# A decoder after three small attentions: the self-attention's keys in three float32r products, their weights' parts made a layer ahead, the feed-forward weights loaded for every pair

## The chip, the core and the metric

The kernel runs on one core of one Trainium2 chip, as one program. The metric is the device time of one execution in microseconds (us), the median of the runs. All data is float32 outside; "float32r" is a rounded form of float32 in which TensorE takes a product in one pass. A float32 matrix is split into a high part (its float32r rounding) and a low part (the rest, again in float32r), and a product is then high·high + low·high + high·low: three float32r products in place of one float32 product.

Engines are called PE (TensorE), DVE (VectorE), ACT (ScalarE), POOL (GpSimd) and SP (SyncE, which only issues DMAs here). POOL issues DMAs too, from its own queue.

## The reference

x is (8, 112, 256), the context (8, 375, 128).

```
x = attend(x, ctx, L0) + x                       # one head of 256, softmax over the 375 context rows
x = layernorm(attend over queries(x, ctx, L1) + x) * gamma + beta     # softmax over the 112 rows
x = attend(x, ctx, L2) + x
for each of 6 layers:                            # 16 heads of 64
    tn = ln(x);  x = mha(tn, tn, sa_kv, sa_q, sa_ow, mask 112x112) + sa_ob + x
    tn = ln(x);  x = mha(ctx, tn, ca_kv, ca_q, ca_ow, context mask) + ca_ob + x
    tn = ln(x);  x = x + relu(tn @ w1 + b1) @ w2 + b2       # 256 -> 1024 -> 256
```

## The kernel before, in words

The batch of 8 is worked in 4 pairs (NB = 2 batches each, 224 token columns). There are three parts, each with its own counts of how often each PSUM bank is filled and emptied (`Place`): the front part (FRONT_LOOP, the three small attentions n = 0, 1, 2, each over the four pairs u), a start (START, the first pair's self-attention of layer 0 and its feed-in), and the main loop (MAIN_LOOP) of 6 x 4 = 24 iterations, one for each layer and pair. In one iteration a pair gets the self-attention's output rows, the cross-attention and the feed-forward network, and, interleaved with it, the next pair gets its self-attention's keys, queries, scores and sums, so that PE has work while other engines do softmax. The order in each engine's queue is written out by hand; engines wait for each other through semaphores.

The pieces that the change touches:

- **Weight parts.** The self-attention's query and value weights are used in the main loop as parts. In the front part, 24 rounds make them, for all layers: SP loads 128 rows of a weight (0.5 MB) into `w_vq` (`load_raw`, line 374, DMA line 376), POOL makes the high part (line 533) and the low part (line 535) (`parts_of_weights`), SP stores both (1 MB) to a tensor in HBM (`store_parts`, DMA line 381) and waits for the store before it issues a load again. Two places of `w_vq` take turns. POOL works off 16 of the 24 rounds ahead of the rstd computations of n = 1 (`PARTS_BEFORE_NORM`, `inverse_std`, line 522, which DVE's normalisation waits for), and 8 behind them. In the main loop POOL issues one load of 2 MB for the queries and one for the values in each iteration (`load_parts`, line 540).
- **Keys.** The next pair's keys, 8 chunks of 128 columns, are plain float32 products of `w_k` (loaded once a layer) and `tnT_next_full`; they are put between the cross-attention's score tiles at the steps t = 1, 2, 3, 4, 6, 7, 9, 10 of 28 (`KEY_STEPS`). The queries' 8 chunks follow at later steps and are already three float32r products (`projected_in_parts`). A score tile t is three float32r products of 376 columns into one of two banks; PE waits, before tile t, until DVE has taken the maximum of tile t - 2 out of its bank (line 1559). DVE's queue for a step is: maximum of t, reciprocal of t - 1, transposition of tile t - 3 (line 1577), and the odd key chunks' copies (line 1411).
- **Feed-forward weights** `f_1`, `f_2` have SBUF of their own and are loaded once a layer, at its last pair's end.
- **POOL in an iteration**: residual plus bias (line 583), the context pair's high and low part (lines 587, 590), rstd after the self-attention (520, 522), a bias (525), the queries' load (540), then 28 multiplications of a tile of probabilities by 1/sum (602), the values' load, and the next self-attention's part.
- **The front part's end.** For n = 1 DVE, pair by pair, adds PE's bank to the residual (line 1372), takes statistics (1270, 1277), and normalises the pair before (`front_normalise`: two `tensor_scalar` of 256 columns, line 1284, a product with gamma and a sum with beta, 512 columns each, lines 1324 and 1326). After n = 2 it copies each pair to `t_all` (1383) and zeroes the masked columns of the context (1388), four times; PE, SP and DVE itself wait for all four (`front_done`). Then the START part's statistics, rstd and normalisation of the first pair follow, and PE's first transposition.

## Time and profile before

| | |
|---|---|
| median of 3 runs | 2946.46 us (2946.38 to 2948.57) |
| the profiled execution: its own time | 2949.26 us |
| its span, first to last instruction | 2947.4 us |
| mean granted TensorE clock | 0.988 |
| PE busy | 2802.5 us (95%), 24232 matmuls |
| DVE / ACT / POOL busy | 58% / 44% / 37% |
| DMA | 248.56 MB, mean 84 GB/s |
| chain that ended last | PE 84%, DVE 5%, DMA 3% |

"Busy" is an engine's time inside instructions; matmuls are pipelined, so PE's 95% is no peak. The chain is followed back from the last instruction to whatever released each step. The main loop starts at about 290.55 us of the span and each of its iterations takes about 110.17 us (POOL's line 583 at 1399.08 and at 1509.23).

### The profile page before, as it was taken

The page shows a single profiled execution, that of the slowest core. Times are in us where ns is not written, and L with a number is a line of the kernel's source. Part 1 is how long each engine was busy: PE and PEld are TensorE (multiplying, and loading weights), DVE is VectorE, ACT ScalarE, POOL GpSimd, SP SyncE. Part 2 cuts the span into 40 slices and gives each one's busy share as a digit, 9 for nine tenths or more (in the row PEclk, how much of TensorE's full clock was granted, in tenths as well). Part 3 has the DMA queues.
Part 4 walks back from the last instruction along what each step waited for, and adds up shares of the span by engine and source line. Part 5 has one row for each costly group of instructions (what it writes and reads, how often), then busy time and mean ns, then how long its engine had stood idle before and what let it go on. Part 6 is the DMA issues. An engine that isn't in the chain of part 4 may idle for free.

```text
span 2947.4 us, 63938 instructions
## 1 busy us (share of the span) xinstructions
PE 2802.5 (95%) x24232; PEld 2340.4 (79%) x24232; DVE 1705.6 (58%) x6436; ACT 1304.4 (44%) x4273; POOL 1082.8 (37%) x1265
## 2 busy tenths in 40 slices
PE   6767999999999999999999999999999999999999
PEld 4545888888888888888888888888888888888887
DVE  2344656656656656656656655655655655655655
ACT  2223445445444444444444444444444444444444
POOL 2552333433433433433433333333333333333333
PEclk9978999999999999999999999999999999999999
DMA  6645022133222133222133222133222133222120
GB/s 202 241 185 189 32 83 58 35 112 98 67 81 58 40 107 99 74 73 57 49 98 99 82 65 58 56 91 99 88 59 58 62 85 101 88 57 57 59 57 14
DMA packets 148055, 248.56 MB, mean 84 GB/s; under 512 B 16733, under 2 KB 122790, under 8 KB 141478
## 3 DMA queue, kind: packets, MB, share of 16 engines
q1 hardware_dynamic: 140838, 143.79, 18.0%
q0 software_dynamic: 6912, 100.67, 9.4%
q8 instruction: 195, 3.19, 0.5%
q14 instruction: 110, 0.90, 0.1%
HBM read 218.35 MB, written 26.08 MB: 83 GB/s over the span
## 4 chain that ended last, share of the span: by engine, by line
PE 84%; DVE 5%; DMA 3%; POOL 2%; issue 2%; SPq 2%; ACT 1%; DVEq 0%; POOLq 0%; ACTq 0%
PE proj L645 18%; PE sum L966 16%; PE score L645 13%; PE proj L665 9%; PE sum L665 9%; PE sum L645 6%; PE proj L987 3%; PE score L819 2%; PE sum L843 2%; PE proj L924 2%; PE tr L830 1%; PE tr L924 1%; POOL rstd L522 1%; PE tr L966 1%; PE proj L637 1%
## 5 line engine op out<-in xcount | busy, mean ns | idle before, releaser
L602 POOL TENSOR_TENSOR prob<-prob,rtotal 128x375 f32<-128x375 f32 x672 | 543.4, 811 | 685.7 <-DVE rtotal L1568 684.7
L1043 ACT ACTIVATE prob<-prob,negmax 128x375 f32<-128x375 f32 (+1 forms) x686 | 417.7, 609 | 444.0 <-DVE negmax L1559 414.1
L966 PE MATMUL sum<-pT,ctx 32*128 32x224 f32 (+1 forms) x4608 | 500.6, 358 | 15.1 <-DVE qcT L1551 15.1
L966 PE MATMUL tr<-pT,ctx 32*128 32x224 f32 (+1 forms) x4608 | 500.7, 358 | 0.0
L966 PEld LDWEIGHTS sum<-pT,ctx 32*128 32x128 f32 (+1 forms) x4608 | 417.9, 185 | 68.3 <-issue 62.8
L1559 DVE CUSTOM_DVE_ANT_0 prob<-score,cbias 128x375 f32<-128x375 f32 x672 | 357.1, 531 | 186.3 <-PE score L645 180.4
L966 PEld LDWEIGHTS tr<-pT,ctx 32*128 32x128 f32 (+1 forms) x4608 | 417.0, 185 | 0.0
L645 PE MATMUL score<-ctx_parts,qc_high 128*128 128x376 f32 x1344 | 390.9, 372 | 0.0
L1577 DVE STREAM_TRANSPOSE pT<-prob 128x384 f32<-128x384 f32 x672 | 372.6, 558 | 0.0
L564 POOL TENSOR_TENSOR prob<-prob,rtotal 112x448 f32<-112x448 f32 x200 | 186.4, 932 | 452.3 <-DVE rtotal L1426 452.3
L1122 ACT ACTIVATE prob<-prob,negmax 112x112 f32<-112x112 f32 x800 | 298.8, 377 | 85.5 <-DVE negmax L1444 85.5
L645 PEld LDWEIGHTS score<-ctx_parts,qc_high 128*128 128x128 f32 x1344 | 222.0, 189 | 59.3 <-issue 57.2
L645 PE MATMUL score<-ctx_parts,qc_low 128*128 128x376 f32 x672 | 224.8, 335 | 0.0
L1444 DVE CUSTOM_DVE_ANT_0 prob<-score,sbias 112x112 f32<-112x112 f32 x800 | 167.3, 270 | 35.4 <-PE score L819 34.9
L645 PE MATMUL proj<-pT,w_k 128*128 128x224 f32 x768 | 176.4, 352 | 0.0
L645 PE MATMUL proj<-tnT,f 128*128 128x224 f32 x768 | 165.1, 363 | 11.0 <-ACT tnT L1104 11.0
L1129 ACT ACTIVATE v<-proj 112x512 f32<-112x512 f32 x50 | 29.9, 598 | 322.2 <-PE proj L645 322.2
L645 PE MATMUL sum<-tnT,c_q 128*128 128x224 f32 x768 | 162.0, 359 | 0.0
L645 PEld LDWEIGHTS proj<-tnT,f 128*128 128x128 f32 x768 | 135.6, 189 | 26.7 <-issue 15.5
L645 PEld LDWEIGHTS sum<-tnT,c_q 128*128 128x128 f32 x768 | 138.6, 189 | 18.4 <-issue 13.3
L1122 ACT ACTIVATION_READ_ACCUMULATOR prob<-prob,negmax 112x1 f32 x800 | 151.4, 189 | 0.0
L645 PEld LDWEIGHTS proj<-pT,w_k 128*128 128x128 f32 x768 | 140.1, 189 | 1.1
(241 smaller groups left out, 5090.4 us busy)
## 6 DMA issues: line engine op xcount, KB each, us to landing
w_vq_parts<-sa_v_parts POOLq DMA_DIRECT2D x24, 2048.0 KB, 9.1
w_vq_parts<-sa_q_parts POOLq DMA_DIRECT2D x24, 2048.0 KB, 8.5
ctx<-ctx SPq DMA_DIRECT2D x192, 176.0 KB
sa_q_parts<-w_vq_parts SPq DMA_DIRECT2D x12, 1024.0 KB, 5.7
sa_v_parts<-w_vq_parts SPq DMA_DIRECT2D x12, 1024.0 KB, 5.2
f<-ff_w SPq DMA_DIRECT2D x12, 1024.0 KB, 8.4
cmask<-ctx_mask SPq DMA_DIRECT2D x24, 375.0 KB, 4.3
w_k<-sa_kv SPq DMA_DIRECT2D x6, 1024.0 KB, 5.5
```

Of the source, the lines that this page charges most:

```text
L564: pool.tensor_tensor(pr, pr, rtotal[0:S, G * g:G * g + G].unsqueeze(2).broadcast_to([S, G, S]), ALU.mult)\
L602: pool.tensor_tensor(row, row, rtotal[:, G * SG + i:G * SG + i + 1].broadcast_to([P, S2]), ALU.mult).then_inc(prob_ready, 1)
L645: ins = pe.matmul(bank[0:w.shape[1], 0:m.shape[1]], w, m, start=k == 0, stop=k == len(weights) - 1)
L665: ins = pe.matmul(bank[0:S, col:col + E], a, w, start=k == 0, stop=k == len(terms) - 1)
L924: ins = pe.matmul(bank[:, i * T2:(i + 1) * T2], c_kT[rows, c + i, :], qcaT[rows, c + i, :], start=True, stop=True)
L966: ins = pe.matmul(bank[:, 0:HT * R], ctx4[keys_of, m // (HALVES // NB), j, :], pT[keys_of, m % 2, :, j * R:(j + 1) * R], start=j == 0, sto ...
L987: ins = pe.matmul(bank[n * D:(n + 1) * D, c % 2 * T2:(c % 2 + 1) * T2], c_v[:, h * D:(h + 1) * D], cT[:, :, h * S:(h + 1) * S], start=True ...
L1043: act.activation(o, i, ACT.Exp, bias=negmax[0:rows, col:col + 1], scale=scale, accum_out=total[0:rows, col:col + 1]).then_inc(exp_ready, 1)
L1122: ins = act.activation(row, row, ACT.Exp, bias=negmax[0:S, col:col + 1], scale=-1.0, accum_out=total[0:S, col:col + 1])
L1444: ins = dve.tensor_tensor_reduce(out=prob[0:S, k % PROBS, h * S:(h + 1) * S], in0=banks[name][0:S, h * S:(h + 1) * S], in1=sbias[:, g // G ...
L1559: dve.tensor_tensor_reduce(out=prob[:, t % PROBS, 0:S2], in0=banks[name][:, 0:S2], in1=cbias[:, t // TB, :], scale=-SCALE, scalar=3.4e38, ...
L1577: dve.transpose(pT[:, m % 2, i % HT, :], prob[:, i % PROBS, 0:S2B]).then_inc(turned, 1)
```

## The change

1. The key weights get parts too, and the keys are three float32r products, like the queries (`projected_in_parts` with `w_kf_parts`). START's keys stay float32, from a raw copy in `stage`.
2. The parts are made a layer ahead: 6 rounds (layer 0: value, query, key weights, two halves each) in the front part, and in each of the layers 0 to 4 two rounds in each of the first three iterations for the layer after, 30 rounds in 15 iterations. They use one small buffer `stage` instead of two places in `w_vq`, so that load, making and store follow one another.
3. `w_kf` holds the key parts or, later in the iteration, `f_1` and `f_2`: the key parts are loaded by POOL at each iteration's start (2 MB, `load_parts(it + 1, "sa_k", ...)`), the feed-forward weights by SP in each iteration once PE has finished the keys (2 x 1 MB).
4. All 6 front rounds stand ahead of n = 1's rstd; `front_normalise` becomes four `scalar_tensor_tensor` of 256 columns for a pair.
5. The context is masked during n = 2, behind DVE's `sum1` copies; the last residual sums go straight to `t_all`; START's first statistics and normalisation stand between them; `front_done` is gone and PE and SP wait for the last sum instead.

```diff
-    IN_PARTS = [(l, name) for l in range(L) for name in ("sa_q", "sa_v")]
-    ROUNDS_OF_PARTS = EK * len(IN_PARTS)
-    PARTS_BEFORE_NORM = EK * 8
+    IN_PARTS = [(l, name) for l in range(L) for name in ("sa_v", "sa_q", "sa_k")]
+    LAYER_ROUNDS = EK * len(IN_PARTS) // L
+    ITERATION_ROUNDS = 2
+    def rounds_in(it):
+        l, p = it // PAIRS, it % PAIRS
+        if l == L - 1 or p * ITERATION_ROUNDS >= LAYER_ROUNDS:
+            return ()
+        first = LAYER_ROUNDS * (l + 1) + ITERATION_ROUNDS * p
+        return tuple(range(first, first + ITERATION_ROUNDS))
-        w_k = sb("w_k", [P, EK, HDIM])
+        w_kf, w_kf_parts = in_one_place("w_kf", "w_kf_parts", [P, 2, EK, HDIM])
+        stage, stage_parts = in_one_place("stage", "stage_parts", [P, 2, HDIM])
+        f_1, f_2 = w_kf[:, 0, :, :], w_kf[:, 1, :, :]...
...
# SP
+            def load_raw(r):
+                (l, which), k = IN_PARTS[r // EK], r % EK
+                if r > 0:
+                    sp.wait_ge(parts_stored, 16 * r)
+                sp.dma_start(stage[:, 1, :], whole_of[which][l, k * P:(k + 1) * P, :]).then_inc(loaded["stage"], 16)
+            def store_parts(r):
+                sp.wait_ge(parts_ready, r + 1)
+                sp.dma_start(stored_parts[IN_PARTS[r // EK]][:, :, r % EK, :], stage_parts[:, :, :].bitcast(f32))...
-            load_w_k(0)
+            load_first(w_vq[:, 1, :, :], "sa_q", "first_w_q")
+            load_first(w_vq[:, 0, :, :], "sa_v", "first_w_v")
+            load_raw(0)
...
-            sp.wait_ge(front_done, PAIRS)
+            for r in range(LAYER_ROUNDS):
+                store_parts(r)
+                if r < LAYER_ROUNDS - 1:
+                    load_raw(r + 1)
+            sp.wait_ge(parts_stored, 16 * LAYER_ROUNDS)
+            load_first(stage[:, :, :], "sa_k", "first_w_k")
+            sp.wait_ge(taken["proj1"], Place(START).emptied("proj1", 0))
...
+                for r in rounds[0:1]:
+                    store_parts(r)
+                    load_raw(r + 1)
                 sp.wait_ge(smask_used, it + 1)
                 load_pair_smask(next_p)
...
+                for r in rounds[1:2]:
+                    store_parts(r)
+                    load_raw(r + 1)
+                sp.wait_ge(ready["proj1"], at.at("proj1", 1 + V2 + QC_FILLS + HC // 2))
+                load_ff(l)
...
-                if p == PAIRS - 2 and l < L - 1:
-                    sp.wait_ge(ready["proj1"], at.at("proj1", Q_END))
-                    load_w_k(l + 1)
-                    load_ff(l + 1)
# POOL, front part and main loop
-            for i in range(PARTS_BEFORE_NORM):
-                parts_of_weights(at, i)
+            for r in range(LAYER_ROUNDS):
+                parts_of_weights(r)
...
                     pool.tensor_tensor(tw[:, :, :], t_all[:, ds(p * NB, NB), :], ...)      # residual plus bias
+                    load_parts(it + 1, "sa_k", "w_k")
+                    pool.wait_ge(ctx_masked, PAIRS)
...                                                                   # the context's high and low part
+                    for r in rounds[0:1]:
+                        parts_of_weights(r)
                     inverse_std(at, 0)
...
                     load_parts(it + 1, "sa_q", "w_q")
+                    for r in rounds[1:2]:
+                        parts_of_weights(r)
                     for i in range(NT):                               # the 28 tiles of probabilities
# PE
-                                pe.wait_ge(loaded["w_k"], (next_layer + 1) * 16)
-                            projected(at, f"proj{c % 2}", w_k, tnT_next_full, c)
+                                pe.wait_ge(loaded["w_k"], (it + 1) * 16)
+                            projected_in_parts(at, f"proj{c % 2}", w_kf_parts, tnT_next_high, tnT_next_low, c)
...
# DVE
                     for b in range(NB):
-                        ins = normalise(ftn[u][:, b, :], ftw[u], b, u)
+                        ins = dve.scalar_tensor_tensor(ftn[u][:, b, :], ftw[u][:, b, :], mv2[:, u, b, 0:1], fbias[0:S, 3, :],
+                                                       ALU.subtract, ALU.mult)
                     link(at, ins)
-                    link(at, dve.tensor_tensor(ftn[u], ftn[u], gamma, ALU.mult))
-                    dve.tensor_tensor(ftw[u], ftn[u], beta, ALU.add).then_inc(tn_ready, 1)
+                    for b in range(NB):
+                        ins = dve.scalar_tensor_tensor(ftw[u][:, b, :], ftn[u][:, b, :], rstd2[:, u, b:b + 1], fbias[0:S, 4, :],
+                                                       ALU.mult, ALU.add)
+                    ins.then_inc(tn_ready, 1)
...
+                    if n == 2:                                        # behind the copy of bank sum1 of pair u
+                        dve.scalar_tensor_tensor(pair_ctx, fcmask[u]..., 0.0, pair_ctx, ALU.not_equal, ALU.mult)...
...
-                    dve.tensor_tensor(ftw[u][:, :, :], bank..., ftw[u][:, :, :], ALU.add).then_inc(taken["proj1"], 1)
+                    dve.tensor_tensor(t_all[:, u * NB:(u + 1) * NB, :] if n == 2 else ftw[u][:, :, :],
+                                      bank..., ftw[u][:, :, :], ALU.add).then_inc(taken["proj1"], 1)
+                    if n == 2 and u == 0:
+                        dve.wait_ge(taken["proj1"], at.emptied("proj1", at.n["proj1"]))
+                        statistics(START_PLACE, first)
+                    if n == 2 and u == 1:
+                        normed(START_PLACE, first)
-            for u in range(NU):                                       # after n = 2
-                dve.tensor_copy(t_all[:, u * NB:(u + 1) * NB, :], ftw[u][:, :, :])
-                dve.scalar_tensor_tensor(pair_ctx, ..., ALU.not_equal, ALU.mult).then_inc(front_done, 1)
-            dve.wait_ge(front_done, PAIRS)
```

## Rows read from the trace of the kernel before

**Rows 1.** Busy time by stretch: us, each engine's busy us (instructions), granted TensorE clock, DMA.
```profile
176.80:182.00 5.20, 5.20 (x15) 4.28 (x16) 0.45 (x1) 0.99 (x2) 4.03 (x3) 0.50 0.00 0
250.95:257.00 6.05, 4.84 (x14) 4.17 (x15) 0.48 (x2) 1.32 (x3) 0.00 (x0) 0.50 1.05 381
290.55:2947.40 2656.85, 2602.44 (x23272) 2193.01 (x23272) 1594.90 (x6125) 1229.64 (x4035) 972.59 (x1176) 1.00 0.24 71
```

**Rows 2.** Timeline of POOL in the front part: start, us, [idle before, releaser].
```profile
56.17 1.04 POOL L533 CAST w_vq_parts<-w_vq 128x1024 fp32r<-128x1024 f32 x1 [13.05 <-DMA w_vq<-sa_q]
57.29 2.35 POOL L535 TENSOR_TENSOR w_vq_parts<-w_vq,w_vq_parts 128x1024 fp32r<-128x1024 f32 x1
...
155.56 2.34 POOL L535 TENSOR_TENSOR w_vq_parts<-w_vq,w_vq_parts 128x1024 fp32r<-128x1024 f32 x1
```

**Rows 3.** DMA issues: count, KB each, median us from issue to landing.
```profile
w_vq_parts<-sa_q_parts POOLq DMA_DIRECT2D x24, 2048.0 KB, 8.5
...
sa_v_parts<-w_vq_parts SPq DMA_DIRECT2D x12, 1024.0 KB, 5.2
...
w_vq<-sa_kv SPq DMA_DIRECT2D x12, 512.0 KB, 4.2
```

**Rows 4.** The chain that ended last, front part, in order of time: start, us, what.
```profile
47.12 9.00 DMA w_vq<-sa_q
...
97.74 6.29 DMA sa_v_parts<-w_vq_parts
...
242.42 0.69 DVE before_low L1372
...
247.00 0.86 DVE ctxT L1388
...
250.95 1.00 PE proj L637 x4
```

**Rows 5.** Timeline of DVE from the end of n = 1.
```profile
130.19 0.69 DVE L1372 TENSOR_TENSOR tw<-proj,tw 112x512 f32<-112x512 f32 x1 [3.19 <-PE proj L767]
...
134.74 0.69 DVE L1372 TENSOR_TENSOR f<-proj,f 112x512 f32<-112x512 f32 x1 [2.69 <-PE proj L767]
...
158.87 0.73 DVE L1284 TENSOR_SCALAR v<-tw,mv,rstd 112x256 f32<-112x256 f32 x2 [22.26 <-POOL rstd L522]
...
167.50 0.69 DVE L1372 TENSOR_TENSOR before_low<-proj,before_low 112x512 f32<-112x512 f32 x1 [2.13 <-PE proj L767]
...
172.43 2.63 DVE L1284 TENSOR_SCALAR w_o<-before_low,mv,rstd 112x256 f32<-112x256 f32 x2
```

**Rows 6.** The chain in the second iteration's key steps, and one query chunk.
```profile
432.73 0.76 PE proj L645 x4
433.49 0.51 PE score L645 x3
...
442.18 0.60 PE score L645 x3
...
443.54 0.51 PE score L645 x3
...
449.45 0.66 PE proj L645 x6
```

**Rows 7.** Timeline of DVE there: the maxima of the tiles t = 4 and t = 9.
```profile
436.73 0.55 DVE L1559 CUSTOM_DVE_ANT_0 prob<-score,cbias 128x375 f32<-128x375 f32 x1 [0.17 <-PE score L645]
...
442.36 0.51 DVE L1559 CUSTOM_DVE_ANT_0 prob<-score,cbias 128x375 f32<-128x375 f32 x1
```

**Rows 8.** Timeline of POOL in a main-loop iteration, from its residual to its probabilities.
```profile
1401.63 1.64 POOL L590 TENSOR_TENSOR ctx_parts<-ctxT,ctx_parts 128x750 fp32r<-128x750 f32 x1 [0.18 <-POOL ctx_parts L587]
1409.25 0.20 POOL L520 TENSOR_TENSOR veps<-mv,eps 112x2 f32<-112x2 f32 x1 [5.98 <-DVE mv L1277]
...
1413.60 0.62 POOL L540 DMA_DIRECT2D w_vq_parts<-sa_q_parts  x1 [1.24 <-PE proj L645]
1426.55 1.58 POOL L602 TENSOR_TENSOR prob<-prob,rtotal 128x375 f32<-128x375 f32 x2 [12.32 <-DVE rtotal L1568]
```

More of the change, by code:

```diff
@@ L458, in _ @@
             load_pair_ctx4(0)
-            load_ff(0)
+            sp.wait_ge(ready["proj1"], Place(START).at("proj1", HC))
+            load_raw(LAYER_ROUNDS)
             for it in range(L * PAIRS):
@@ L465, in _ @@
                 new_layer = p == PAIRS - 1 and l < L - 1
+                rounds = rounds_in(it)
                 if new_layer:
@@ L555, in _ @@
                 add_bias(fbias[0:S, 1, :], ftw[u])
-            for i in range(PARTS_BEFORE_NORM, ROUNDS_OF_PARTS):
-                parts_of_weights(at, i)
             def normalise_group(at, g):
@@ L775, in _ @@
             at.check()
-            pe.wait_ge(front_done, PAIRS)
+            pe.wait_ge(taken["proj1"], Place(START).emptied("proj1", 0))
             def normed(at, n, name, a=tn):
@@ L852, in _ @@
             chunked(at, w_vq[:, 1, :, :], tnT_next, range(G))
-            pe.wait_ge(loaded["w_k"], 16)
-            chunked(at, w_k, tnT_next, range(G))
+            pe.wait_ge(loaded["first_w_k"], 16)
+            chunked(at, stage, tnT_next, range(G))
             emptied(at, "proj0", "proj1")
@@ L857, in _ @@
             chunked(at, w_vq[:, 1, :, :], tnT_next, range(G, HC))
-            chunked(at, w_k, tnT_next, range(G, HC))
+            chunked(at, stage, tnT_next, range(G, HC))
             emptied(at, "proj0", "proj1")
@@ L1284, in normalise, with normed @@
                 return dve.tensor_scalar(o, a[:, b, :], mv2[:, u, b, 0:1], rstd2[:, u, b:b + 1], ALU.subtract, ALU.mult)
+            def normed(at, a, o=tn):
+                wait_rstd(at)
+                for b in range(NB):
+                    normalise(o[:, b, :], a, b).then_inc(tn_ready, 1)
+            START_PLACE = Place(START)
+            first = t_all[:, 0:NB, :]
             dve.wait_ge(setup_done, 1)
@@ L1458, in attended @@
                     .then_inc(taken["sum1"], 1)
-            at = Place(START)
-            first = t_all[:, 0:NB, :]
-            statistics(at, first)
-            normed(at, first)
+            at = START_PLACE
             new_smask(0)
```

80 lines of the change are left out of this document (31 added, 49 removed).

## The prediction

> **What bounds the kernel now.** I read the page first: PE is busy 95% and holds 84% of the chain that ended last. Then the stretches: from 290.55 us to the end PE is busy 2602 of 2657 us at full clock [rows 1], so in the 24 main-loop iterations a saving counts where it shortens PE's queue, as long as no other engine is as tight in that place. The other 290 us, the front part, are another matter. There DVE stood still for 22.3 us before it could normalise the first pair of n = 1, for POOL's rstd [rows 5]; and POOL was not computing rstd, it was making weight parts, whose 16th round ended at 157.9 us [rows 2]. The rounds' pace is SP's and the DMAs': load, make, store [rows 2 to 4]. So the front part is bound, between 136.6 and 158.9 us, by work that nothing there needs.
>
> I count from the profiled execution: 2949.26 us, span 2947.4. It lies 2.8 us above the median of the runs shown, which is taken off at the end.
>
> **The change part by part.**
>
> *Rounds ahead of the rstd, 16 to 6.* A round makes its parts in 1.04 + 2.35 us and a gap of 0.1, say 3.5 [rows 2]. With one buffer a round is load + make + store in a row: 4.2 + 3.5 + 5.2 = 12.9 us with the median landings [rows 3], and some 0.5 for SP's issues, 13.4. The first load now stands behind two 1 MB loads, but two raw loads and the 1 MB of keys stood there before; I leave its parts ready at 59.7 us [rows 2]. The sixth is then ready at 59.7 + 5 x 13.4 = 126.7. DVE first wants an rstd at 158.87 - 22.26 = 136.6 [rows 5]. So the wait goes: 22.3 us. It would begin to come back from a round of (136.6 - 59.7) / 5 = 15.4 us on.
>
> *What is late next.* DVE's sums of the pairs come 134.74 - 130.19 = 4.55 us apart when nothing waits [rows 5], PE with one bank being the pace. Without the stall the fourth comes at 134.74 + 2 x 4.55 = 143.8 instead of 167.50: 23.7 us, the extra 1.4 being PE's products, which ran at half clock after its stop.
>
> *Fused normalisation.* From the fourth sum to PE's last transposition of n = 2 (about 176.8) the trace has 9.3 us. New: the sum 0.7, statistics 1.2, and for two pairs 4 fused instructions each. No row shows this form. Below it lies half of the 0.73 us that two `tensor_scalar` take, above it the 0.69 us of a two-source sum twice as wide [rows 5]; I take 0.40, near the lower, since the width is 256 in both. That is 3.2 us, with links 5.4, so an end at 149.2. But the trace's last `tensor_scalar` pair took 2.63 instead of 0.73 us while POOL added the biases [rows 5], and this overlap stays: I add 2. 151.2 against 176.8 - 23.7 = 153.1 gives 1.9 us (0 to 4).
> The Trainium skill speaks against the fusion: VectorE: DVE Perf Modes, Mode 2×_2P, says that a single-source float32 operation between SBUF places can do two elements a cycle and one with a second tensor cannot, so two fast instructions are given up. By its formula for a two-tensor float32 sum (the section before the tier table), an estimate of (256 + 151) / 0.96 = 424 ns, the eight would take 3.4 us and the sum would lose 0.2.
>
> *The clock in n = 2.* PE starts n = 2 at half clock, 5.2 us between 176.8 and 182 [rows 1], after gaps that the last normalisations leave. They get shorter, not gone. All of it back is 2.6 us, none is 0; I take 1.3.
>
> *Masking the context in n = 2* puts 0.86 us on DVE four times [rows 4] beside PE's sums. The last one stands ahead of the first copy of the values' projection; I charge 0.4 (0 to 3.4 if nothing covered them).
>
> *The front part's end.* PE's first transposition of START began at 250.95, DVE's last sum ended at 242.42 + 0.69 = 243.1 [rows 4]. In between lay the copies, masks, statistics, rstd and normalisation. The statistics and the normalisation of the first pair now lie between sums in which DVE waits about 2 us for PE each, and rstd takes POOL one of the three gaps. PE can go at 243.2: 7.7 us. PE then has no long stop before it, and the half clock from 250.95 to 257, 4.84 us of work [rows 1], falls away: 2.4 us (0 to 2.4). SP's loads of START move by the same amount and have the whole of START.
>
> Front part: 23.7 + 1.9 + 1.3 - 0.4 + 7.7 + 2.4 = 36.6 us (30 to 42).
>
> *Keys in three products.* A key chunk takes PE 0.76 us, a query chunk of the same size in parts 0.66 [rows 6]. Eight chunks, 24 iterations: 0.10 x 192 = 19 us if PE alone sets the pace. It doesn't. In this stage DVE waited for PE only once, 0.17 us at t = 4 [rows 7], and PE already waited for DVE: the tile t = 10 took 0.60 instead of 0.51 in the chain [rows 6], at its wait for the maximum of t = 8. Of the 23 iterations from the second on, 22 have that one wait of 0.16 or 0.17 us and no other there. Walking the two queues with 0.66: DVE ends the maximum of t = 9 at 442.9 - 0.17 = 442.7; PE waits for it at t = 7, 9 and 10 and would start t = 11 at 443.0 instead of 443.54 [rows 6]. So 0.5 of the 0.8 us stays. Behind t = 11 come the sums, where DVE waits for PE again, so it is kept: 24 x 0.5 = 12.2 us. Bounds: 0.17 an iteration, 4 us, if PE follows DVE all the way; 19 us if DVE never binds.
>
> *In the main loop at nothing*: the key parts' load, issued by POOL at an iteration's start in 0.62 us and landed 8.5 us later [rows 3, 8], is wanted some 30 us later; behind it POOL's context parts slip by 0.6 and have 20. The feed-forward load (2 MB) is issued after the keys and wanted 50 us later. Without that cover each would cost up to its 8.5 us, 24 times.
>
> *Two rounds of parts in 15 iterations.* The first: POOL ends the context's low part at 1403.3, with the load 1403.9, with a round 1407.4; its rstd is wanted at 1409.25 [rows 8]. Free by 1.8 us. SP then stores (5.2), loads (4.2), 0.6 for issues: 1417.4. POOL's second round ends at 1420.9; the first probabilities come at 1426.55 [rows 8]. Free by 5.6 us. What queues behind it is the multiplication of the tiles, then DVE's transpositions and PE's context sums.
> DVE in these two windows only takes PE's banks and small pieces. The Trainium skill, SBUF — State Buffer, Who interferes with whom, says that DVE and GpSimd share one pair of ports, and that only a DVE instruction in a 2-port mode or with two SBUF inputs contends with GpSimd. By that rule the rounds cost DVE nothing there; the 2.63 us row agrees with its other half.
>
> Sum: 36.6 + 12.2 = 48.8. 2949.3 - 48.8 = 2900.5; as a median, 2.8 less: **2897.7 us**.
>
> **Rivals.** (A) is the forecast, 2888 to 2909.
> (B) *DVE is not tight*: PE gets its 19 us, and with warm clocks 40 in front: 2946.5 - 59 = 2887. For it: PE's waits in the stage are few and short. Against: DVE's single 0.17 us.
> (C) *The key stage is DVE's*: 4 us there, 2906. For it: DVE's queue has no gap after t = 4. Against: PE works out 0.3 us ahead at t = 11.
> (D) *One buffer makes the front rounds slow*: with the slowest landings of the trace, 9.0 and 6.3 [rows 4], a round is 18.8 us, the sixth ends at 153.7, and 17 us of the wait stay: 2915. Decides from 15.4 us a round.
> (E) *The second round in an iteration holds up the probabilities.* With one landing at 9.0 it ends at 1426 to 1427, 0.3 to 1.3 us late, 15 times: about 2911. Slower than before it gets if the raw piece queues behind the queries' 2 MB, issued at 1413.6 [rows 8]: 8.5 + 9.0 makes 1431.1, the round ends 1434.6, 8.1 us late, 15 x 8.1 = 121 us, 3019 in all. It costs from a piece later than 1423.0, and turns the sign from 3.3 us more. Against: HBM and queues are near idle there (mean 71 GB/s in the loop [rows 1], 2 MB in 8.5 us is 245).
> (F) *The change doesn't bring float32r's price*, since 6 short products load weights 6 times: the query chunk shows 0.66 with them, so the loop would keep its time only if the key weights' new place did something that the query weights' doesn't: 2910.
>
> **How the numbers follow.** Two kernels a fifth of a per cent apart (5.9 us) can't be told apart here. A 0.55, B 0.13, C 0.12, D 0.06, E mild 0.06, E slower 0.04, F 0.02, and 0.02 for no change by several of them at once. Faster: 0.94, same 0.02, slower 0.04. The range 2884 to 2913 reaches B and mild E and leaves out D and slow E.
>
> **What would show it.** After: DVE's wait for rstd before its first n = 1 normalisation is under 1 us, and the sixth round ends before 136 us; START's first transposition comes 8 us earlier than its front part's shift, at full clock; an iteration takes 109.6 to 109.8 us instead of 110.17, alike with and without rounds (a difference between p = 3 and the others is E); key chunks take 0.66 in the chain, with PE waits for DVE's maxima between. I am wrong if the loop's iterations don't shorten, or if another wait stands at n = 1's end in place of the rstd.

## The result and the profile after

| | before | after |
|---|---|---|
| median of 8 runs, us | 2948.14 (2946.38 to 2950.69) | 2956.42 (2950.49 to 2962.55) |
| ratio | | 1.0028, 95% interval 1.0016 to 1.0039 |
| profiled execution (span), us | 2949.26 (2947.4) | 2950.49 (2948.5) |
| start of the main loop, us | 290.55 | 255.00 |
| from there to the end, us | 2656.85 | 2693.50 |
| most iterations that make no parts, us | 110.17 | 110.02 |
| the 15 that now make parts, us | 110.1 to 110.5, the first 116.6 | 111.3 to 114.9, the first 119.5 |

The forecast was 2897.7 (2884 to 2913), so it was wrong by 59 us and on the sign. The front part gave 35.55 us of the 36.6 that were forecast. The main loop took 36.65 back. It should have given 12. The last iteration takes 115.4 us before and 115.2 after. The profiled execution of the kernel after is the fastest of its eight runs, 5.9 us under their median, so the loss in its trace is smaller than the usual one.

The start of an iteration is read from POOL's residual, line 598 now (583 before); two starts apart is an iteration's length. The stretches that answer to [rows 1], the kernel after: time, busy time of PE, weight loads, DVE, ACT and POOL, granted clock, DMA share, GB/s.

```profile
154.38:159.58 5.20, 5.20 (x15) 4.28 (x16) 0.45 (x1) 0.99 (x2) 1.27 (x1) 0.50 0.00 0
216.36:222.41 6.05, 4.84 (x18) 4.34 (x19) 0.65 (x2) 1.32 (x4) 0.00 (x0) 0.72 0.82 264
255.00:2948.50 2693.50, 2611.56 (x23656) 2187.32 (x23656) 1607.28 (x6125) 1229.12 (x4035) 1080.68 (x1260) 0.99 0.38 119
```

PE is 9 us busier than before although its key products got shorter, and it stands still for 82 us instead of 54. Who it waits for is in the view of waits. After (engine, line, released by: us in total, times, longest):

```profile
PE sum L665 <- DVE oT L1564: 26.3, 16, 3.0
DVE sbias L1444 <- DMA smask<-self_mask: 26.2, 15, 3.4
```

Neither line exists in the trace before. `new_smask` turns the next pair's self-attention mask into a bias; in DVE's program it stands between the second values copy and the first of the cross-attention query copies (`oT` is the name that shares `qcaT`'s place), and PE needs these copies. The mask's load is on SP's queue. SP in one such iteration, which began at 1382.05 (start, us, engine, line, what):

```profile
1390.00 0.53 SPq L393 DMA_DIRECT2D sa_k_parts<-stage_parts  x1
1394.29 0.35 SPq L389 DMA_DIRECT2D stage<-sa_kv  x1
1394.69 0.43 SPq L370 DMA_DIRECT2D smask<-self_mask  x1
```

DVE in the same iteration:

```profile
1396.33 0.69 DVE L1436 COPY v<-proj 112x512 f32<-112x512 f32 x1 [1.73 <-PE proj L665]
1398.64 1.03 DVE L1444 TENSOR_SCALAR sbias<-smask 112x224 f32<-112x224 int32 x1 [1.62 <-DMA smask<-self_mask]
1399.82 0.39 DVE L1564 COPY oT<-sum 128x224 f32<-128x224 f32 x1
```

and PE in a worse one, which began at 1153.20:

```profile
1167.30 2.43 PE L665 MATMUL sum<-tnT,c_q 128*128 128x224 f32 x12
1172.68 1.02 PE L665 MATMUL sum<-tnT,c_q 128*128 128x224 f32 x4 [2.95 <-DVE oT L1564]
1173.64 1.59 PE L944 MATMUL proj<-oT,c_kT 64*128 64x224 f32 x8
1175.16 2.85 PE L665 MATMUL sum<-tnT,c_q 128*128 128x224 f32 x8
...
1178.90 1.78 PE L665 MATMUL sum<-tnT,c_q 128*128 128x224 f32 x8
```

In before the mask was issued 96 us into the iteration before, as soon as its place was free (at a layer's end 9.3 us into the iteration, behind the output weights). Now `store_parts(r)` stands ahead of it and waits for POOL's round (8 us into the iteration), and `load_raw(r + 1)` waits for the store to land (12.2 us in). The mask goes out at 12.6, behind 512 KB of raw weights, lands 3.9 us later and is wanted at 15. In the worse iteration PE stood for 2.95 us and then ran for a while at half clock: eight products of c_q took 2.85 instead of 1.78, and the stretch around them has a mean granted clock of 0.70:

```profile
1175.16:1178.90 3.74, 3.74 (x18) 3.00 (x16) 1.55 (x3) 1.33 (x3) 0.00 (x0) 0.70 0.75 301
```

The iterations in which PE stood 1.0 to 1.7 us lost 1.3 to 2.0; those in which it stood 2.1 to 3.0 lost 4.0 to 4.9.

### The profile page after: what moved, and what is told of

The parts are those of the page before. It is cut to its first block, busy times and chain, and to the rows that moved or that the text cites. A ratio compares the mean times of both kernels' runs of the same rounds, so it can differ in the third digit from the quotient of the medians.

```text
span 2948.5 us, 64849 instructions
## 1 busy us (share of the span) xinstructions
PE 2807.1 (95%) x24616; PEld 2329.9 (79%) x24616; DVE 1713.6 (58%) x6432; ACT 1304.0 (44%) x4273; POOL 1129.8 (38%) x1313
## 4 chain that ended last, share of the span: by engine, by line
PE 81%; DVE 6%; POOL 5%; DMA 4%; issue 2%; ACT 2%; SPq 0%; DVEq 0%; POOLq 0%; ACTq 0%
PE proj L665 18%; PE sum L986 16%; PE score L665 13%; PE proj L685 7%; PE sum L685 7%; PE sum L665 5%; PE proj L1007 3%; PE score L839 2%; DMA smask<-self_mask 2%; PE sum L863 2%; PE proj L944 2%; PE tr L850 1%; PE tr L944 1%; POOL stage_parts L549 1%; PE proj L657 1%
## 5 line engine op out<-in xcount | busy, mean ns | idle before, releaser
L665 PE MATMUL score<-ctx_parts,qc_high 128*128 128x376 f32 x1344 | 368.2, 355 | 0.0
L665 PEld LDWEIGHTS score<-ctx_parts,qc_high 128*128 128x128 f32 x1344 | 209.2, 189 | 62.7 <-issue 53.4
L665 PE MATMUL sum<-tnT,c_q 128*128 128x224 f32 x768 | 171.1, 369 | 26.3 <-DVE oT L1564 26.3
L665 PE MATMUL proj<-tnT,w_kf 128*128 128x224 f32 x768 | 165.1, 363 | 10.9 <-ACT tnT L1124 10.9
L665 PEld LDWEIGHTS proj<-tnT,w_kf 128*128 128x128 f32 x768 | 135.6, 189 | 26.7 <-issue 15.4
L1063 ACT ACTIVATION_READ_ACCUMULATOR prob<-prob,negmax 128x1 f32 (+1 forms) x686 | 128.0, 187 | 0.0
L665 PEld LDWEIGHTS score<-ctx_parts,qc_low 128*128 128x128 f32 x672 | 126.2, 188 | 0.0
```

The costliest lines, as they stand in the source:

```text
L665: ins = pe.matmul(bank[0:w.shape[1], 0:m.shape[1]], w, m, start=k == 0, stop=k == len(weights) - 1)
L1063: act.activation(o, i, ACT.Exp, bias=negmax[0:rows, col:col + 1], scale=scale, accum_out=total[0:rows, col:col + 1]).then_inc(exp_ready, 1)
```

## The experiments

Every run has runs of before on the same chip beside it. Most iteration lengths repeat between runs within 0.03 us, and they are compared across chips here; those quoted are the usual ones of a run's trace.

### Mask first

The changed kernel, two statements of SP exchanged:

```diff
+                sp.wait_ge(smask_used, it + 1)
+                load_pair_smask(next_p)
                 for r in rounds[0:1]:
                     store_parts(r)
                     load_raw(r + 1)
-                sp.wait_ge(smask_used, it + 1)
-                load_pair_smask(next_p)
```

> The changed kernel with two statements of SP's queue exchanged: the load of the next pair's self-attention mask stands ahead of the first round's store and raw load again, instead of behind them. Nothing else differs. Theory 1 (the mask comes late because it is queued behind a store that waits for POOL's round, and DVE's in-order queue then holds up the query copies that TensorE needs): the mask wait goes in all 18 iterations that have rounds, these iterations fall from 110.8 to 119.5 us to 110.0 to 110.7, the main loop from 2693.5 to about 2653 to 2660, and the time to 2908 to 2916 us. Rival (the rounds themselves, by the port that POOL shares with DVE or by their extra 1.5 MB of transfers, make these iterations long): they stay at 111 to 115 us and the time stays above 2935.

Measured: 2913.15 us (2911.01 to 2915.07), ratio to before 0.9883 (0.9866 to 0.9899). The iterations with rounds behind the first are 110.0, one of them 110.3. The loop is 2656.50 us, 37.0 less than in the changed kernel. (The iterations with rounds are 15, not the 18 that the expectation says.) The waits of this kernel, in the same view:

```profile
DVE sbias L1444 <- DMA smask<-self_mask: 1.3, 1, 1.3
PE sum L665 <- DVE oT L1564: 1.0, 2, 0.6
```

25.3 of the 37.0 us are PE's wait. The rest is PE's busy time, 2611.56 us in the changed kernel's loop against 2599.63 here, for the same 23656 instructions. Most of that is half clock. In the stretch from 16 to 26 us into an iteration the changed kernel's granted clock is 0.83 in five iterations (the 9th, 10th, 13th, 17th and 19th, those with the stops of 2.1 us and more) and 1.00 in all others behind the first. A mean of 0.83 over 10 us is 3.4 us at half clock, 1.7 us lost, so some 8.5 us in five iterations, as an estimate; the last 3 us are open.

### No rounds

The mask-first kernel without any round in the main loop: every layer takes the parts of layer 0, so layers 1 to 5 compute with the wrong weights.

```diff
-        if l == L - 1 or p * ITERATION_ROUNDS >= LAYER_ROUNDS:
+        if True:
             return ()
...
-            load_raw(LAYER_ROUNDS)
...
-                pool.wait_ge(parts_stored, 16 * LAYER_ROUNDS * (l + 1))
+                pool.wait_ge(parts_stored, 16 * LAYER_ROUNDS)
...
-                pool.dma_start(o[:, :, :, :], stored_parts[l, which]).then_inc(loaded[name], 16)
+                pool.dma_start(o[:, :, :, :], stored_parts[0, which]).then_inc(loaded[name], 16)
```

> The kernel of the mask-first run without any round of weight parts in the main loop: POOL makes none, SP neither loads raw rows nor stores parts, and every layer's queries, keys and values take the parts of layer 0, so that layers 1 to 5 compute with the wrong weights; all other transfers and all arithmetic of TensorE stay. Theory 1: the rounds cost next to nothing once the mask is in time, so the iterations are 110.0 us and the time is 0 to 8 us below the mask-first run (0 to 0.4 us per iteration with rounds, for DVE instructions slowed by the shared port). Rival (rounds cost by themselves): 15 to 45 us below it.

Measured: 2912.96 us (2910.34 to 2914.38) against 2913.15. The iterations that had rounds are 110.0 us with and without them, except the first, which is 118.85 instead of 119.56; three at a layer's end came to 110.6 to 111.2, where DVE waited up to 1.3 us for a mask behind the output weights. The rounds by themselves cost next to nothing, as the prediction said of them. What they did to SP's queue was the cost.

### Late mask in the kernel before

```diff
                 sp.wait_ge(smask_used, it + 1)
+                sp.wait_ge(resid_ready, at.at("resid", 2))
                 load_pair_smask(next_p)
```

> The kernel before with one wait added on SP's queue: the next pair's self-attention mask is loaded only after POOL's second bias addition (resid_ready at 2, some 13 us into the iteration) instead of during the previous one. No rounds, no key parts. Theory 1 (a mask load issued this late holds up DVE's query copies and by them TensorE, and that alone lengthens the iteration): iterations grow from 110.17 by 1.3 to 4.3 us, the time by 30 to 100 us to 2978 to 3048. Rival (the late mask cost only beside POOL's rounds): within 8 us of before.

Measured: 2947.30 us, ratio 0.9997 (0.9988 to 1.0007): no change. The theory was wrong in this form. The mask went out 13.4 us into the iteration, later than in the changed kernel, and still came all but in time: DVE waited 0.3 to 0.8 us for it and PE not at all. The DMA views of this run and of the changed kernel, from 500 to 2700 us, have for it (KB, median us from issue to landing):

```profile
smask<-self_mask SPq DMA_DIRECT2D x20, 98.0 KB, 1.9
```
```profile
smask<-self_mask SPq DMA_DIRECT2D x19, 98.0 KB, 3.9
```

The issue time is only half of it; 2 us more are in what goes ahead of it. Two runs for that.

### Mask between store and raw load

The changed kernel, the mask issued once the store has landed, the raw load behind it:

```diff
                 for r in rounds[0:1]:
                     store_parts(r)
-                    load_raw(r + 1)
+                    sp.wait_ge(parts_stored, 16 * (r + 1))
                 sp.wait_ge(smask_used, it + 1)
                 load_pair_smask(next_p)
+                for r in rounds[0:1]:
+                    load_raw(r + 1)
```

> The changed kernel with the mask's load between the landing of the first round's store and the raw load that follows it: it is issued only some 0.4 us earlier than in the changed kernel, about 12.2 us into the iteration, but ahead of the 512 KB raw load instead of behind it. Theory 1 as refined by the late-mask run (the late issue alone is harmless, a mask issued 13.4 us in and landed 2 us later cost nothing; what costs is the raw load's transfer ahead of it on the same queue, which makes the mask land after 3.9 us): iterations with rounds are 110.0 to 110.6 us and the time 2909 to 2918. Rival (the issue time decides, 2 us later than POOL's and SP's other work allows): iterations stay at 111 to 115 us and the time above 2935.

Measured: 2914.28 us (one run). In the iteration that began at 1365.35 SP's rows are

```profile
1377.60 0.32 SPq L370 DMA_DIRECT2D smask<-self_mask  x1
1377.96 0.46 SPq L389 DMA_DIRECT2D stage<-sa_kv  x1
```

12.25 us in, 0.39 earlier than in the changed kernel, and its iterations with rounds are 110.0 to 110.6. The mask lands in 2.1 us here. So 0.4 us of issue and the place ahead of 512 KB together are worth all but about 1 us of what mask-first brings.

### Late mask behind a 512 KB load, in the kernel before

```diff
                 sp.wait_ge(smask_used, it + 1)
+                sp.wait_ge(resid_ready, at.at("resid", 2))
+                if it > 0:
+                    again = min(l + (p + 1) // PAIRS, L - 1)
+                    sp.dma_start(w_k[:, 1, :], dec["sa_kv"][again, P:2 * P, 0:HDIM]).then_inc(w_k_again, 16)
                 load_pair_smask(next_p)
...
```

(PE waits for `w_k_again` at its first key chunk.)

> The kernel before with its mask load held to 13.4 us into the iteration, as in the late-mask run, and a 512 KB load (one chunk of the key weights once more, from the second iteration on) issued on SP's queue just ahead of it. No rounds, no key parts. Refined theory 1: the mask now lands some 4 us after its issue instead of 2.0, DVE waits 1.5 to 4 us for it, and iterations grow from 110.17 by 0.7 to 4.5 us, the time by 16 to 100 us to 2963 to 3048. Rival (POOL's rounds beside it are needed for the loss): within 8 us of before.

Measured: 3017.52 us (one run), iterations from the second on of 112.3 to 112.8 us and six of 113.6 to 116.3. No round and no key part is in this kernel's main loop, and it shows the changed kernel's loss, greater still since no iteration is spared. Its waits:

```profile
DVE sbias L1425 <- DMA smask<-self_mask: 67.4, 24, 3.7
PE sum L649 <- DVE oT L1548: 51.5, 23, 3.0
```

Here too the loss, 2607.66 against 2541.42 us over 23 iterations, is larger than PE's wait. The cause is shown from both sides: the mask issued late and behind a long transfer of its own queue. No run has the 512 KB ahead of the mask on another queue, so it isn't shown that they must be on the same one; the run with the late key load below has a mask that is slower still with 2 MB beside it on POOL's queue. The Trainium skill, DMA: Bandwidth & Descriptors, Queues, rings and completion order, says that each queue has one ring per DMA engine, consumed in ring order, while an engine takes turns between queues. The trace agrees with it: behind 512 KB of its own queue the mask took 3.9 and 4.0 us, without it 1.9 and 2.1.

### Short key copies, and keys copied by ScalarE

Both are the mask-first kernel. In the first, DVE copies 16 of 224 columns of each odd key chunk (the keys are left incomplete). In the second, ScalarE copies the odd chunks too.

```diff
                         if KEY_STEPS.get(t, 0) % 2 == 1:
-                            keys(at, KEY_STEPS[t])
+                            chunk(at, kT[:, KEY_STEPS[t], 0:16], 16)
```

> The kernel of the mask-first run, with DVE's copy of each odd key chunk in the main loop cut from 224 to 16 columns, so that the self-attention keys of the odd chunks are left incomplete; TensorE does the same work. Theory 2 (the context tiles with key chunks are bound by DVE, where a tile costs a maximum, a reciprocal, a transpose and half a key copy, 1.15 us on average, against 1.05 on TensorE, so that what the three-product form saves on TensorE is not seen): four copies of 0.36 us become about 0.1 us, and an iteration without rounds falls from 110.02 by 0.3 to 0.9 us, the time by 7 to 20 us against the mask-first run. Rival (the gain of the keys is lost elsewhere, at the wait of TensorE for ScalarE's copy or at the clock): less than 0.1 us per iteration, under 3 us in all.

```diff
# DVE
-                            keys(at, KEY_STEPS[t])
+                            at.next("proj1")
# ScalarE, behind its even chunks
+                        if KEY_STEPS.get(t, 0) % 2 == 1:
+                            c = KEY_STEPS[t]
+                            act.wait_ge(ready["proj1"], at.at("proj1", 1 + V2 + QC_FILLS + c // 2 + 1))
+                            act.activation(kT[:, c, :], banks["proj1"][:, 0:T2], ACT.Copy).then_inc(taken["proj1"], 1)
```

> The kernel of the mask-first run, with the four odd key chunks of the main loop copied by ScalarE (0.34 us each) instead of DVE (0.36). Theory 2 (DVE is the bound of this stage): the iteration falls by 0.2 to 0.8 us as long as ScalarE, with an exponential of 0.61, its accumulator read of 0.19 and now nearly one copy a tile, 1.07 us a tile, keeps pace; 5 to 19 us in all against the mask-first run. Rival (ScalarE's copies come later than DVE's, since they stand behind the exponential of the tile, and TensorE waits for the bank): the iteration grows by 0.1 to 1 us.

Measured: 2906.79 us (2905.05 to 2908.98) and 2905.92 (2903.59 to 2906.92), iterations 109.74 and 109.73 instead of 110.01. That is 6.4 and 7.2 us under mask-first; the first is a little under its forecast of 7 to 20, the second within 5 to 19, and both are clear of the rivals. DVE's copies were what held the stage.

### Keys in float32 again, with either way of copying

```diff
-                            projected_in_parts(at, f"proj{c % 2}", w_kf_parts, tnT_next_high, tnT_next_low, c)
+                            projected(at, f"proj{c % 2}", w_kf_parts[:, 0, :, :].bitcast(f32), tnT_next_full, c)
```

> The kernel of the mask-first run with the main loop's key chunks in two float32 products again (on the rounded upper parts of the weights), the copies shared between ScalarE and DVE. It undoes the keys alone; all transfers stay. Theory 2 (DVE binds this stage in either form): the iteration goes back from 110.0 to 110.1 to 110.25 us, the time up by 2 to 6 us against 2911 to 2915. Rival (a TensorE saving of 0.10 us a chunk does arrive and something else in the loop took it back): 110.5 to 110.9.

> The same keys in two float32 products, with all eight key chunks copied by ScalarE. With three float32r products and these copies the iteration was 109.73 us, with the copies shared 110.01. Theory 2: with DVE relieved (1.00 us a tile) TensorE's 0.76 us a chunk binds, so the float32 form gains little from it, 110.0 to 110.25 us an iteration, and the three-product form is then worth 0.3 to 0.5 us an iteration instead of 0.15. Rival (the 0.28 us came from somewhere else than the interplay of DVE and the key chunks): the float32 form gains the same 0.28 and comes to about 109.87.

Measured: 2917.48 and 2914.80 us (one run each). The iterations make a table of four:

| iteration, us | copies shared | copies by ScalarE |
|---|---|---|
| keys in float32 | 110.18 | 110.06 |
| keys in three float32r products | 110.01 | 109.73 |

The change alone brings 0.17 us an iteration, the other copying alone 0.12, both 0.45. Each hides behind the other. The chain of the changed kernel's key stage in an iteration without rounds answers to [rows 6] (start, us, what):

```profile
2640.65 0.52 PE score L665 x3
2641.17 0.82 PE proj L665 x6
2642.00 0.52 PE score L665 x3
2642.52 0.66 PE proj L665 x6
...
2644.88 0.58 PE score L665 x3
2645.46 0.66 PE proj L665 x6
2646.12 1.27 PE score L665 x6
2647.40 0.66 PE proj L665 x6
2648.06 0.69 PE score L665 x3
```

A key chunk takes 0.66, as forecast. What it saves comes back in the score tiles, 0.58 and 0.69 instead of 0.52 and 1.27 for two instead of 1.04, where PE waits for DVE's maxima, and once (0.82) in its wait for ScalarE's copy. DVE behind it:

```profile
2643.18 0.16 DVE L1590 RECIPROCAL rtotal<-total 128x1 f32<-128x1 f32 x1
2643.26 0.56 DVE L1599 STREAM_TRANSPOSE pT<-prob 128x384 f32<-128x384 f32 x1
2643.74 0.35 DVE L1436 COPY kT<-proj 128x224 f32<-128x224 f32 x1
2644.01 0.53 DVE L1581 CUSTOM_DVE_ANT_0 prob<-score,cbias 128x375 f32<-128x375 f32 x1
...
2644.48 0.16 DVE L1590 RECIPROCAL rtotal<-total 128x1 f32<-128x1 f32 x1
...
2645.04 0.51 DVE L1581 CUSTOM_DVE_ANT_0 prob<-score,cbias 128x375 f32<-128x375 f32 x1
```

Its queue is without a gap here. From one tile's reciprocal to the next it needs 1.30 us with a copy (2643.18 to 2644.48) and 1.00 without; PE needs 1.18 for a tile with a key chunk. With all copies on ScalarE the maxima from t = 6 on are 1.00 us apart.

### Six rounds in the kernel before

The front part alone: 6 rounds instead of 24 (EK is 2, so the 12 and 48 of the expectation are twice the counts), all ahead of the norm, and the main loop takes the parts of layer 0 (layers 1 to 5 compute with the wrong weights).

```diff
-    ROUNDS_OF_PARTS = EK * len(IN_PARTS)
-    PARTS_BEFORE_NORM = EK * 8
+    ROUNDS_OF_PARTS = EK * 3
+    PARTS_BEFORE_NORM = EK * 3
...
```

> The kernel before with 12 rounds of weight parts in the front part instead of 48, all of them ahead of the layer norm's statistics; the main loop takes the parts of layer 0 in every layer, so layers 1 to 5 compute with the wrong weights. The norm in DVE and ScalarE, the masking and the end of the front part stay as before. Theory of the forecast (the wait for the reciprocal deviation is 23.7 us and the reordered end of the front part another 7.7, with 1.9 of the fused norm): the main loop starts 22 to 28 us earlier than 290.55, at 262 to 269, against 255 with the whole change. Rival (all of the gain is POOL's and the queue's, and the reordering is worth nothing): it starts at 253 to 258.

Measured: the loop starts at 262.01 us (the time is 2920.93, one run). Fewer rounds alone are worth 28.5 us, half a us more than the forecast's 22 to 28; the rival's start at 253 to 258 did not come. The remaining 7.0 to the changed kernel's 255.00 are a net: the reordered end (7.8), START (1.1), n = 2 (2.2) and the fused norm (0.3) give 11.4 us against this run, and 4.4 are lost because n = 1's sums come later in the changed kernel (the fourth at 145.43 us, here at 141.06). Why they come later is open.

### The version with both, and the first iteration

Mask first with ScalarE's key copies, timed again:

> The best version so far once more, timed in more rounds: mask load first, all key chunks copied by ScalarE. Both theories expect 2904 to 2907 us, a ratio to before of 0.985 to 0.987.

Measured: 2906.11 us (2903.60 to 2908.48), ratio 0.9856 (0.9839 to 0.9872). Its first iteration is 119.6 us, that of before 116.6. There the main loop's first POOL instructions meet DVE's splitting of the normed tokens. In that version, POOL's key load was moved behind its split of the context:

```diff
-                    load_parts(it + 1, "sa_k", "w_k")
                     pool.wait_ge(ctx_masked, PAIRS)
 ...
                         .then_inc(split_ready, 1)
+                    load_parts(it + 1, "sa_k", "w_k")
```

> The best version so far with POOL's load of the key parts issued behind its split of the context parts instead of ahead of it. Theory (the 3 us by which the first iteration is longer than before, 119.6 to 119.9 against 116.6 us, come from POOL being at work while DVE casts the normed tokens): the first iteration falls by 0.5 to 2 us, the others stay at 109.73, so the time falls by 0 to 2 us. Rival (the first iteration is long because of the transfers of the key parts and of the raw rows): no change.

Measured: 2919.67 us (2918.88 to 2921.67), 13.6 slower. The first iteration did fall, to 117.21, but the five at a layer's end, which have no rounds, rose to 111.5 to 114.2. SP and DVE in the one that began at 594.19:

```profile
603.00 0.39 SPq L396 DMA_DIRECT2D w_o<-sa_ow  x1
603.43 0.58 SPq L370 DMA_DIRECT2D smask<-self_mask  x1
```
```profile
611.50 0.28 DVE L1448 TENSOR_SCALAR sbias<-smask 112x224 f32<-112x224 int32 x1 [2.34 <-DMA smask<-self_mask]
```

The mask again, now behind the 1 MB of output weights. That order is old, and the mask went out at the same 9.2 us into the iteration as before; but with the key parts' 2 MB issued 4.1 instead of 1.2 us in, it took 8.0 us to land instead of 5.5. Two runs told the two effects apart: the late key load in the first iteration alone (`if it == 0` there, `if it > 0` in the old place), and the late key load in all with the mask ahead of everything on SP in the iteration.

> The version with the mask first and ScalarE's key copies, with POOL's load of the key parts behind its split of the context parts in the first iteration alone. Theory (the first iteration's 3 us and the new-layer iterations' loss are two separate effects of the moved load): the first iteration is 117.0 to 117.5 us, all others 109.7 to 110.2, and the time is 2 to 3 us below that version's 2906. Rival (the first iteration's gain belongs to another start of the front part): 119.6 again and no change.

> The key-load-after-split kernel (the load moved in every iteration), with the self-mask's load ahead of the output weights' load in the five iterations at a layer's end. Theory (in those iterations it was the mask again, which stands behind 1 MB of output weights on its queue and beside 2 MB of key parts on the other): they fall from 111.5 to 114.2 us to 109.7 to 110.2, and the time from 2920 to 2902 to 2906. Rival (the later key load itself, or the output weights landing late beside it): they stay above 111 us.

Measured: 2903.67 us (2902.68 to 2904.85), ratio 0.9848 (0.9833 to 0.9863), first iteration 117.23, the others 109.7 to 110.1; and 2905.88 (2900.67 to 2907.17), first iteration 117.24, the layer ends 109.7 to 109.8. Both as the theory had them. The first of the two is the best version: 44.0 us under before on the same chip, some 53 under the changed kernel's median. The first iteration's rows for DVE, mask-first kernel and best version:

```profile
254.26 3.33 DVE L1429 CAST tnT_next_high<-pT 128x224 fp32r<-128x224 f32 x2
257.74 2.01 DVE L1432 TENSOR_TENSOR tnT_next_low<-pT,tnT_next_high 128x448 fp32r<-128x448 f32 x1
```
```profile
253.19 2.00 DVE L1436 CAST tnT_next_high<-pT 128x224 fp32r<-128x224 f32 x2
255.34 1.00 DVE L1439 TENSOR_TENSOR tnT_next_low<-pT,tnT_next_high 128x448 fp32r<-128x448 f32 x1
```

They take 5.3 and 3.0 us for the same work, and 3.0 in before too. With the mask first and ScalarE's copies they still take 5.3, so the place of POOL's key load makes the difference. It accounts for 2.3 of the 2.9 us by which the changed kernel's first iteration is longer.

## Why the prediction was wrong, by its steps

The profiled executions, term by term (us; minus is faster):

| term | forecast | measured |
|---|---|---|
| front part | -36.6 | -35.55 |
| keys | -12.2 | -3.3 |
| first iteration | 0 | +2.9 |
| rounds in the loop: self-mask's load | 0 | +37.0 |
| sum | -48.8 | +1.05 (spans 2947.4, 2948.5) |

The keys' and the first iteration's terms are the mask-first kernel's loop against before's (110.01 against 110.17 on average, 119.57 against 116.63), the last is the changed kernel's loop against the mask-first one's. By the medians the kernel is 8.3 us slower and not 1.05, and the mask's term is 43 (2956.42 against 2913.15), since the profiled execution is the fastest of its eight.

*The step that failed: "Two rounds of parts in 15 iterations".* It timed POOL's queue right (the rstd began at 10.2 us into the iteration with 2.27 us to spare, the second round ended at 1402.0 with the first probabilities at 1411.5) and named what stands behind the round on POOL. It used SP's store and load for their durations only and never asked what else stands behind them on SP. In these iterations `store_parts` is the first instruction on SP's queue, it waits for POOL's round, and the mask's load stands behind it and the raw load. None of the rivals has the mask. E came nearest, a landing that is late for an in-order engine, but placed it at POOL's probabilities, and that wait did not come.

*Front part.* DVE's rows after that answer to [rows 5]:

```profile
131.75 0.69 DVE L1407 TENSOR_TENSOR tw<-proj,tw 112x512 f32<-112x512 f32 x1 [3.19 <-PE proj L787]
...
138.10 0.85 DVE L1350 SCALAR_TENSOR_TENSOR v<-tw,mv,before_low 112x256 f32<-112x256 f32 x2
...
145.43 0.69 DVE L1407 TENSOR_TENSOR before_low<-proj,before_low 112x512 f32<-112x512 f32 x1 [0.89 <-PE proj L787]
...
148.21 1.91 DVE L1354 SCALAR_TENSOR_TENSOR before_low<-c_q,rstd,before_low 112x256 f32<-112x256 f32 x2
150.04 2.89 DVE L1350 SCALAR_TENSOR_TENSOR w_o<-before_low,mv 112x256 f32<-112x256 f32 x2
```

The wait for rstd is gone (138.10), and the sums are 4.56 us apart, as forecast (4.55). The sixth round ended at 112.9, where 126.7 was forecast: the first ended at 54.6 instead of 59.7, and the next came every 11.0 to 13.1 us, not 13.4. The first sum is 1.56 us later than in before (131.75 against 130.19), so 22.1 came of 23.7. The fused norm gave 0.3 instead of 1.9: an instruction takes 0.44 us where 0.40 was taken, and beside POOL's bias additions 0.96 and 1.45, which the flat 2 us for that overlap was too little for. The end of the front part gave 7.8 for 7.7: START's first transposition begins at 216.36, right behind DVE's last sum (215.62 + 0.69). START itself gave 1.0 for 2.4; its first 6 us are at clock 0.72, not full (second row of the stretches). n = 2 gave 4.4 for 0.9, but elsewhere than forecast. The half clock at its start stayed as it was (0.50 in the first row of the stretches). The gain is in its transpositions and context sums, which have ahead and now:

```profile
210.63:226.35 15.72, 13.26 (x73) 12.40 (x72) 5.53 (x16) 4.04 (x12) 9.15 (x6) 0.67 0.62 230
```
```profile
188.21:199.45 11.24, 8.91 (x74) 8.31 (x72) 6.94 (x18) 4.14 (x12) 0.00 (x0) 1.00 0.00 0
```

Before, POOL was busy 9.15 us there with rounds, PE stood for DVE's and ScalarE's copies up to 1.75 us and ran at a mean clock of 0.67; now POOL does nothing and the clock stays full. POOL's rounds explain only a part of it. In the kernel before with six rounds POOL does nothing there either. That gave 1.7 us, in the transpositions; its context sums ran at 0.65 and took 8.01 us all the same, where before took 7.80 and the changed kernel 5.40:

```profile
189.68:197.69 8.01, 8.01 (x49) 8.01 (x49) 1.33 (x4) 1.06 (x4) 0.00 (x0) 0.65 0.00 0
```

PE's longest stop ahead of them is 1.32 us in both, so why the clock falls in one and stays full in the other is open. The front part's misses cancel: 22.1 + 0.3 + 4.4 + 7.8 + 1.0 = 35.6. That the sum came within about 1 us of the forecast is luck, since 3.5 of it is a gain in n = 2 that nothing in the prediction foresaw.

*Keys.* Rival C was right: DVE's stage, 0.14 to 0.17 us an iteration. The mis-sized term is the distance from DVE's maximum to the score tile that waits for it. In the chain a tile takes 0.52 us when nothing holds it, so the tile t = 7 above, which ends at 2645.46, began at 2644.94, and its maximum had ended at 2644.54 (2644.01 + 0.53): 0.4 us. It is 0.3 for t = 9 and 0.4 for t = 10, and 0.4 in before for t = 10. The walk of the two queues used little over 0.1: t = 11 at 443.0 puts t = 10 at 443.0 - 0.66 - 0.52 = 441.82, and the maximum of t = 8, which ended at 441.87 in before, would have ended 0.17 earlier, at 441.70. With 0.4 in its place t = 11 comes at 443.3 and some 0.3 us is left of the 0.5. The trace shows 0.20: from the first key chunk to t = 11 it is 10.61 us here (2638.80 to 2649.41) and 10.81 in before (432.73 to 443.54). ScalarE's copy of the first key chunk, 0.16 us late now, was not in the walk at all.

*At nothing.* The key parts' load (8.4 us) and the feed-forward's (7.0) stay hidden in the loop, as said. The exception is the first iteration, where START's end, not a loop iteration, lies ahead of POOL, and where moving POOL's key load alone gave 2.3 us.

*Slips in the working.* 24 x 0.5 is 12.0, not 12.2. And the mild form of E has no price: with a landing of 9.0 instead of 4.2 the round would end at 1420.9 + 4.8 = 1425.7, ahead of the 1426.55 at which it is wanted. Neither moves the forecast by more than 0.2 us.

*The signs it named.* No wait for rstd, the sixth round ahead of 136 us, key chunks of 0.66 with PE's waits between: these came. Iterations without rounds are 110.02 us and not 109.6 to 109.8, and START's first transposition came 7.8 us ahead of its shift but at clock 0.72. The iterations with rounds did differ from those without; the prediction had kept that sign for E, and it was the mask.

*The chances.* 0.94 for faster was far too sure. The rivals were variations on the waits that I had listed, and the list was short by one queue.

## What to carry to other kernels

When an instruction that waits is put on a queue, write down the whole queue behind it, with the engine that waits for each entry and how much time it has. On a DMA queue an entry can be late twice, by its issue and by the bytes ahead of it; small loads that an in-order engine wants soon go ahead of long ones. And where two engines are within a few per cent of each other in a stage, relieving one brings little, relieving both brings more than the sum of the two.

## What the runs showed of the hardware

- A DVE instruction, once started, can take three times as long beside POOL: the mask's bias took 1.03 us instead of 0.34 while POOL made parts (in the first iteration 1.45 with rounds and 0.34 in the run without), a fused instruction of the norm 1.45 instead of 0.43 beside bias additions. The prediction had let the rounds cost DVE nothing. The Trainium skill, SBUF — State Buffer, Who interferes with whom, covers the first by its rule on `tensor_scalar`, which can take both port pairs, and the second by its rule on two SBUF inputs; the rows agree. It was small in sum: without rounds the loop was no faster.
- PE's longer stops can cost more than their length: in the changed kernel 2.95 us of standing came with a 4.86 us longer iteration, 1.70 with 1.97. There half clock followed all five stops of 2.1 us and more and none of the nine up to 1.7. That is no fixed border: in the run with the late mask behind a load it followed a stop of 2.31 us, but not one of 2.35 or one of 3.02, and the last cost 3.3 us in all.
- The spread of the runs tells little by itself. The changed kernel's eight runs lay 12 us apart and those of before beside them 4, but 13 runs of before on another chip lay 12 us apart too.
